# Two tiles of a layer's gathers replaced by products of adjacency blocks, in a graph network's second layer

## The reference

```python
deg = segment_sum(ones, dst)                 # with a loop at each node
dinv = rsqrt(deg);  norm_edge = dinv[src] * dinv[dst]
for W, b in ((W1, b1), (W2, b2), (W3, b3)):
    msg = (h @ W)[src] * norm_edge[:, None]
    h = relu(segment_sum(msg, dst) + b)
out = layernorm(x + h)
```

## Time and profile before

| | |
|---|---|
| median of three runs | 2339.77 us (2338.68 to 2342.82) |
| the profiled execution | 2341.41 us |
| its span, from its first to its last instruction | 2339.7 us, mean granted TensorE clock 0.972 |
| TensorE busy in matmuls, over the span | 2150.6 us, 92% |
| GpSimd busy, over the span | 1696.3 us, 73% |
| ScalarE, VectorE busy | 740.3 us (32%), 867.4 us (37%) |
| moved in all | 551.88 MB, 236 GB/s |

### The profile page before, as it was taken

How to read it: one execution, slowest core, us unless ns; L and a number is a source line. 1 busy time by engine, 2 the same in 40 slices (tenths; PEclk the granted TensorE clock), 3 DMA queues, 4 the chain that set the end, 5 groups by cost and what they waited for, 6 DMA issues and landing times.

```text
span 2339.7 us, 33336 instructions
## 1 busy us (share of the span) xinstructions
PE 2150.6 (92%) x10765; PEld 1430.9 (61%) x10765; DVE 867.4 (37%) x1213; ACT 740.3 (32%) x1578; POOL 1696.3 (73%) x1768
## 2 busy tenths in 40 slices
PE   5777999999999998899998999999899899999998
PEld 4755677777777774444444444444444368888886
DVE  8888322222222212233333333333332234444443
ACT  7611222323332312232322323322231134444443
POOL 4177777777777776777777777777777777777774
PEclk9788999999999999999999999999999999999999
DMA  7445767667766676888887888888888788888995
GB/s 229 142 122 183 235 201 210 207 210 211 209 206 208 209 210 194 246 259 264 258 261 250 258 264 257 262 245 255 260 257 278 230 259 264 266 265 295 313 317 163
DMA packets 238443, 551.88 MB, mean 236 GB/s; under 512 B 39676, under 2 KB 110451, under 8 KB 238307
## 3 DMA queue, kind: packets, MB, share of 16 engines
q0 software_dynamic: 124608, 395.36, 56.0%
q1 hardware_dynamic: 91011, 121.92, 15.2%
q10 hardware_dynamic: 22688, 32.75, 4.3%
HBM read 463.88 MB, written 86.00 MB: 235 GB/s over the span
## 4 chain that ended last, share of the span: by engine, by line
PE 58%; POOL 16%; issue 13%; DMA 7%; DVE 5%; POOLq 1%; ACTq 0%; DVEq 0%; ACT 0%; SPq 0%
POOL rows L778 15%; PE ps_acc L1756 8%; PE ps_o L1812 7%; PE ps_T L1851 7%; PE ps_h L1851 7%; PE ps_acc L1752 6%; PE ps_d L1862 6%; PE ps_d L1756 6%; DMA rows<-table,idx 5%; PE ps_h L1801 3%; DVE big L941 1%; PE ps_acc L1745 1%; PE ps_acc L1748 1%; PE ps_d L1748 1%; PE ps_d L1745 1%
## 5 line engine op out<-in xcount | busy, mean ns | idle before, releaser
L778 POOL DMA_INDIRECT rows<-table,idx x1018 | 985.3, 968 | 328.9 <-issue 292.0
L1756 PE MATMUL ps_acc<-rows,sel 128*128 128x512 f32 (+2 forms) x1122 | 496.3, 570 | 81.8 <-DMA rows<-table,idx 60.8
L778 POOL DMA_INDIRECT rows<-table_parts,idx x483 | 457.0, 946 | 147.2 <-issue 136.8
L998 DVE SCALAR_TENSOR_TENSOR sel<-ps_e,firsts,dstT 128x1152 f32<-128x1152 f32 (+1 forms) x174 | 246.1, 1414 | 614.5 <-PE ps_acc L1756 213.9
L1756 PE MATMUL ps_d<-rows,sel 128*128 128x512 f32 (+1 forms) x850 | 411.0, 607 | 34.9 <-DMA rows<-table,idx 34.8
L1756 PEld LDWEIGHTS ps_acc<-rows,sel 128*128 128x128 f32 x1122 | 206.6, 202 | 233.4 <-issue 143.7
L778 POOL DMA_INDIRECT rows_r<-table_pairs,idx x231 | 220.0, 952 | 72.1 <-issue 65.3
L1812 PE MATMUL ps_o<-low,hT 128*128 128x512 f32 (+1 forms) x784 | 270.5, 488 | 0.5 <-ACT hT L1432 0.5
L1752 PE MATMUL ps_acc<-rows,sel 128*128 128x256 bf16 (+1 forms) x1533 | 242.8, 274 | 16.9 <-DVE acc L1088 8.3
L1756 PEld LDWEIGHTS ps_d<-rows,sel 128*128 128x128 f32 x850 | 147.5, 191 | 171.2 <-issue 116.0
L1525 ACT ACTIVATE rows_r<-low 128x1280 fp32r<-128x1280 uint8 (+3 forms) x140 | 175.3, 1252 | 187.2 <-PE ps_T L1851 77.2
(11 more groups left out here) (211 smaller groups left out, 2122.8 us busy)
## 6 DMA issues: line engine op xcount, KB each, us to landing
rows<-table,idx POOLq DMA_INDIRECT x1018, 4.0
low<-built ACTq DMA_DIRECT2D x40, 320.0 KB, 4.9
table<-made SPq DMA_DIRECT2D x49, 256.0 KB, 3.1
acc<-table SPq DMA_DIRECT2D x49, 256.0 KB
table_pairs<-made_r SPq DMA_DIRECT2D x49, 256.0 KB
built<-big SPq DMA_DIRECT2D x30, 384.0 KB, 3.7
low<-built_bytes ACTq DMA_DIRECT2D x72, 160.0 KB, 4.0
built_bytes<-big SPq DMA_DIRECT2D x54, 192.0 KB, 4.9
```

The lines of the kernel that those rows point to most:

```text
L778: pool.indirect_dma_start(out=to, out_offset=None, in_=its[0:nodes, :], in_offset=bass.IndirectOffsetOnAxis(ap=idx[:, of, k:k + 1], axis=0 ...
L998: v.scalar_tensor_tensor(to[:, k:k + FRONT, :], numbers.unsqueeze(1).broadcast_to([P, FRONT, P]), firsts[:, bass.ds(t, 1)], dstT[:, bass.d ...
L1756: return mm(to[:, 0:w], sel[:, k, :], rows_of[phase][:, k, 0:w] if first is None else first, start=start, stop=stop)
```

## The change

Tiles 44 and 45 of layer 2 are no longer gathered. Their sums are made in windows 1 to 43, in 49 steps (h = 0 to 48). A step multiplies two 128x128 blocks of counts (one of each tile) with tile h of the layer's table (128x512, fp32) and adds into two PSUM banks, `ps_h` and `ps_o`. A window has one step, at slots 11 and 12 of its order; the six windows without a build have a second one, at 14 and 15. The table's tile is loaded from HBM by SP a window ahead, into two buffers. The counts are loaded in strips of six blocks for each tile, also two buffers, and widened from bf16 to fp32 by ScalarE, one activation of 128x256 a step, between the scaling of a sum and the copies of the build steps. Buffers lie in parts of the build buffers that layer 2, building bytes, leaves unused.

`ps_o` being taken, the products with W3 write into `ps_T`, the bank of the transposes. So it is the turn that now waits for the pair of the product before, and a product waits for all of `hT` at once. `make` and `make_pair` read `ps_T`.

The windows of layer 2 are 0 to 43 and three more, for tiles 46, 47 and 48. The one for tile 46 starts afresh. Turn and product of 44 and 45 are put into the windows of 46 and 47, beside those of the tile before. In layer 3 the two banks of the dense tiles are `ps_h` and `ps_o`, where they were `ps_T` and `ps_h`.

```diff
+AT_2 = (11, 14)
+TWO_PLACES = (3, 7, 7)
+DENSE_2 = (44, 45)
+STRIP = 6
+    GATHER_2 = T - len(DENSE_2)
+    WINDOWS = [0, GATHER_1, GATHER_1 + GATHER_2]
-        ps_dense = [ps_T[:, :], ps_h[:, :]]
+        ps_dense = [ps_h[:, :], ps_o[:, :]]
...
+        TWICE = [ROUND * i + o + 1 for i in range(ROUNDS) for o in range(ROUND) if half_in(o) is None]
+        STEPS_2, at_step = [[]], 0
+        for i in range(1, DENSE_2[0]):
+            STEPS_2.append(list(range(at_step, at_step + (2 if i in TWICE else 1))))
+            at_step += len(STEPS_2[i])
...  SP
+                    def strip(q):
+                        if q > 1:
+                            sp.wait_ge(widened_2, STRIP * (q - 1))
+                        lo_h, hi_h = q * STRIP, min((q + 1) * STRIP, T)
+                        for d, t in enumerate(DENSE_2):
+                            sp.dma_start(strips[:, q % 2, d, 0:(hi_h - lo_h) * P],
+                                         built[(t - GATHER) * P:(t - GATHER + 1) * P, lo_h * P:hi_h * P]).then_inc(strips_in[q % 2], 16)
+                    def loads_2(i):
+                        for h in STEPS_2[i]:
+                            if h > 1:
+                                sp.wait_ge(dense_2_step, h - 1)
+                            sp.dma_start(rows_2[:, h % 2, :], table[1][h * P:(h + 1) * P, :]).then_inc(rows_2_in[h % 2], 16)
+                            if h % STRIP == 0 and 0 < h and h + STRIP < T:
+                                strip(h // STRIP + 1)
...
                                 own_rows(t)
+                                loads_2(t + 1)
                                 stores(i, o, first)
                                 store(t - 1, nth(1, t - 1))
...
+                        strip(0)
+                        strip(1)
+                        loads_2(1)
                         round_of(0, True)
...  VectorE
-                v.scalar_tensor_tensor(made_r[:, C:2 * C], ps_o[:, 0:C], dinv[:, t:t + 1], made_r[:, 0:C].bitcast(F32),
+                v.scalar_tensor_tensor(made_r[:, C:2 * C], ps_T[:, 0:C], dinv[:, t:t + 1], made_r[:, 0:C].bitcast(F32),
...
+                last_pairs = [(DENSE_2[0] - 3,), (DENSE_2[0] - 2, DENSE_2[0] - 1), DENSE_2, (DENSE_2[1] + 1,)]
...
+                            v_.wait_ge(dense_2_step, T)
...  ScalarE
+            def scale_dense_2(d):
+                s = nth(1, DENSE_2[d])
+                act.wait_ge(dense_2_step, T)
+                act.wait_ge(turned, s)
+                act.sem_inc(act_step, 1)
+                nc.scalar.activation(aggT[:, 0:HID], ps_dense[d], ACT.Copy, scale=dinv[:, DENSE_2[d]:DENSE_2[d] + 1]).then_inc(agg_ready, 1)
+            def widen_2(h):
+                act.wait_ge(strips_in[h // STRIP % 2], 32 * (h // STRIP // 2 + 1))
+                if h > 1:
+                    act.wait_ge(dense_2_step, h - 1)
+                act.sem_inc(act_step, 1)
+                at = h % STRIP * P
+                nc.scalar.activation(counts_2[:, h % 2, :, :], strips[:, h // STRIP % 2, :, at:at + P], ACT.Copy).then_inc(widened_2, 1)
...
+            def tile(phase, t, n, s, per, built_half=None, between=None):
+                scale(phase, t, n, s, per)
+                if phase == 1 and per == 1:
+                    for h in STEPS_2[t + 1] if t + 1 < len(STEPS_2) else []:
+                        widen_2(h)
+                behind_scale(phase, t, s, per, built_half, between)
...  TensorE
-            def turn(phase, s, of=agg, at=0):
+            def turn(phase, s, of=agg, at=0, pairs=0):
                 pe.wait_ge(agg_ready, s + 1)
+                if pairs > 0:
+                    pe.wait_ge(pair_made, pairs)
...
-            def product(phase, s, pairs=0):
+            def product(phase, s, to=ps_o):
...
-                if pairs > 0:
-                    pe.wait_ge(pair_made, pairs)
+                if to is ps_T:
+                    pe.wait_ge(hT_ready, KH * s + KH)
...
+                def dense_2(h, d):
+                    if d == 0:
+                        pe.wait_ge(rows_2_in[h % 2], 16 * (h // 2 + 1))
+                        pe.wait_ge(widened_2, h + 1)
+                    ins = mm(ps_dense[d], counts_2[:, h % 2, d, :], rows_2[:, h % 2, :], start=h == 0, stop=h == T - 1)
+                    if d == 1:
+                        ins.then_inc(dense_2_step, 1)
+                def flow_beside(t):
+                    def beside(k):
+                        at = ORDER.index(k)
+                        if at == 10:
+                            turn(1, nth(1, t), aggT if t in DENSE_2 else agg, pairs=t)
+                        if at == 14:
+                            product(1, nth(1, t), ps_T)
+                    return beside
...
+                i = DENSE_2[0]
+                steady(1, i, TWO_PLACES, flow_beside(i), s=nth(1, i - 1), ps=ps_sums[(WINDOWS[1] + i) % 2], afresh=5, tile=tile_in(i))
+                i += 1
+                steady(1, i, TWO_PLACES, flow_beside(i + 1), s=nth(1, i), ps=ps_sums[(WINDOWS[1] + i) % 2], tile=tile_in(i), of=aggT)
+                i += 1
+                steady(1, i, LAST_PLACES[1], s=nth(1, T - 2), ps=ps_sums[(WINDOWS[1] + i) % 2], tile=tile_in(i))
```

More of the change, by code:

```diff
@@ L449, in gnn_program @@
         dense_taken = sem("dense_taken")
+        rows_2_in = [sem(f"rows_2_in{b}") for b in range(2)]
+        strips_in = [sem(f"strips_in{b}") for b in range(2)]
+        widened_2 = sem("widened_2")
+        dense_2_step = sem("dense_2_step")
         res_d_in = sem("res_d_in")
@@ L508, in in_bytes, with tile_in @@
             return not DENSE - DENSE_1 - 1 <= j < DENSE - 1
+        def tile_in(i):
+            return i if i < DENSE_2[0] else i + len(DENSE_2)
+        TWICE = [ROUND * i + o + 1 for i in range(ROUNDS) for o in range(ROUND) if half_in(o) is None]
[3 more added lines that the diff above has]
+            at_step += len(STEPS_2[i])
+        assert at_step == T and DENSE_2[0] == ROUND * ROUNDS + 2 and GATHER_2 == DENSE_2[0] + 3
+        assert all(not in_bytes(t - GATHER) for t in DENSE_2)
         def nth_window(phase, t, per, w):
@@ L692, in phases @@
                             round_of(i)
[L693 to L701, removed]
+                        last_flows = [(DENSE_2[0] - 2,), (DENSE_2[0] - 1, DENSE_2[0]), (DENSE_2[1], DENSE_2[1] + 1), (T - 2,)]
+                        for o, flows in enumerate(last_flows):
+                            i = ROUND * ROUNDS + o + 1
+                            own_rows(tile_in(i), nth_of_windows(1, i), late=i < GATHER_2 - 1)
+                            if o < 2:
+                                stores(ROUNDS, o)
+                            for t in flows:
+                                store(t, nth(1, t))
                         store(T - 1, nth(1, T - 1))
@@ L858, in one_window @@
                     else:
-                        with pool.Fori(0, (GATHER_1, T, GATHER)[phase] // 2) as i:
+                        with pool.Fori(0, (GATHER_1, DENSE_2[0] - 1, GATHER)[phase] // 2) as i:
                             two(i)
+                        if phase == 1:
+                            for i in range(DENSE_2[0] - 1, GATHER_2):
+                                t = tile_in(i)
+                                need = pool.value_load(need_i[0:1, t:t + 1], min_val=0, max_val=99)
+                                window(1, nth_of_windows(1, i), nth_of_windows(1, i) % 2, need, afresh=i == DENSE_2[0])
             def sweeps():
@@ L1178, in one_window, with steady @@
             def one_window():
[L1179 removed]
+                def steady(phase, t, odd, hots=None, whole=None, units=None, last=False, in_parts=False, tile=None, next_tile=None, dense=None, pairs=()):
                     n = nth_of_windows(phase, t)
@@ L1199, in steady @@
                     prepare(n, t, base, 1, sel_parts if in_parts else sel_r if phase == 2 else sel)
-                    if phase == 1 and t > 1:
-                        make_pair(t - 2)
+                    for made_tile in pairs:
+                        make_pair(made_tile)
                 def to_next(phase):
@@ L1446, in make @@
                 act.wait_ge(o_done, s + 1)
+                of = ps_T if phase == 1 and per == 1 else ps_o
                 if phase == 1 and per == 1:
@@ L1614, in first_pieces @@
                         widen(0, x)
-                for t in range(ROUND * ROUNDS, T):
-                    tile(1, t, nth_of_windows(1, t), nth(1, t), 1, between=first_pieces if t == T - 1 else None)
+                for t in range(ROUND * ROUNDS, DENSE_2[0] - 1):
+                    tile(1, t, nth_of_windows(1, t), nth(1, t), 1)
+                t = DENSE_2[0] - 1
+                scale(1, t, nth_of_windows(1, t), nth(1, t), 1)
+                behind_scale(1, t, nth(1, t), 1)
+                scale_dense_2(0)
+                behind_scale(1, DENSE_2[0], nth(1, DENSE_2[0]), 1)
+                scale_dense_2(1)
+                behind_scale(1, DENSE_2[1], nth(1, DENSE_2[1]), 1)
```

(2 more changed lines are left out.)

77 lines of the change are left out of this document (48 added, 29 removed).

## The result

The changed kernel takes 2303.88 us in the median of four runs (2302.12 to 2304.87); the kernel before took 2341.3 us in four runs beside it. The ratio is 0.9836, with a 95% interval from 0.9824 to 0.9848: 37.4 us or 1.6% faster, where 2306 us was forecast. The profiled execution spans 2301.9 us at a mean granted clock of 0.981.

What follows compares the result with a forecast made beforehand. GpSimd's gathers were taken to bound layer 2, TensorE close behind: 2341.4 us, less 38 for gathers removed, plus 4 for the longer stretch, less 1.6 from profiled execution to median, gave 2306 us, range 2300 to 2327.

Steps and rivals of the forecast that it cites:

- GpSimd bounds layer 2, and the gain is its gathers: Layer 2: GpSimd issues gathers without pause, one every 1.260 us; 31 fewer save 36.5 to 39.1 us, 38 taken.
- 91 us free on TensorE, not 62: Windows 1 to 43: TensorE's counted work is 777 of 868 us, leaving 91 free; its busy row shows only 62.
- the window without waits: Layer 2, 1004.04 to 1022.38 us before the change: TensorE waited for nothing, 18.34 us product to product, used for pricing.
- Dense steps, 84.4 us, hidden: Windows 1 to 43: 98 added matmuls at 0.861 us cost TensorE 84.4 us, covered by its 91 free.
- Widening, 7 us of TensorE: ScalarE, before the build copies: 49 activations of 0.5 us delay TensorE by 4 to 14 us, 7 taken.
- Shared bank, nothing: Layer 2's turn, waiting for the pair of the previous product: about 3.4 us in hand with builds, so no cost.
- Loads hidden: SP's queue in layer 2: 16.1 MB of added block and strip loads make no store later.
- the transfers' rival: Layer 2: SP's loads delay gathers if engines sustain under 265 GB/s; 62 us more at 258, 2364 us; chance 0.11.
- Start, 2 us of TensorE, nothing for GpSimd: Window 0: 1.05 MB of loads leaving at once delay TensorE 0 to 4 us, 2 taken, GpSimd not at all.
- The end, hidden: Windows of 46 and 47: turn and product of tiles 44 and 45 are hidden by GpSimd; uncovered, 4.2 us.
- The sum, 872 for the stretch: Windows 1 to 43: TensorE 870 us, GpSimd 868, so about 872 where 868 stood, +4 (bounds 0 and +16).
- nothing lost: Whole kernel, rival: TensorE keeps within GpSimd's pace, the lag absorbed; 2301 us (2298 to 2302), chance 0.10.

Runs made afterwards that it cites:

- relieving TensorE of 81 us: Changed kernel without the matmuls of 47 of the 49 dense steps, their loads and widening kept: 2303.07 us, 0.9847 of the kernel before.
- relieving GpSimd of 58: Changed kernel without the gather of slot 14 in 46 windows of layer 2, stale rows multiplied instead: 2292.55 us, 0.9799 of the kernel before.
- the loaded kernel: Changed kernel with the product of tile 44 made twice in each dense step, 42.2 us more TensorE work: 2336.8 us, 0.9991 of the kernel before.
- the changed kernel's repeat: The changed kernel run again without any edit, as base for the other runs: 2302.28 us, 0.9836 of the kernel before.
- the doubled loads: Changed kernel with 45 of the 49 table blocks loaded a second time into an unused buffer, 11.8 MB more: 2307.73 us, 0.9861 of the kernel before.
- the kernel with early strips: Changed kernel with the first two count strips of both tiles loaded at layer 1's end instead of during window 0: 2305.26 us, 0.9847 of the kernel before.

## Why the prediction was right, step by step

- **GpSimd bounds layer 2, and the gain is its gathers.** Right. From the first gather of layer 2 to the first of layer 3, GpSimd took 996.05 us for 787 gathers before and 959.08 us for 756 after: 31 fewer, 37.0 us less, between the two ways of 36.5 and 39.1; 38 was taken. Relieving TensorE of 81 us changed nothing, and relieving GpSimd of 58 gave 10 us of time, and no more because TensorE stood there.
- **91 us free on TensorE, not 62.** Right, and the step on which the sign hung. The relieved GpSimd let TensorE's work be seen: 860.4 us, against 861.4 from the window without waits. By the busy row 22 us would have been lost; none were. The Trainium skill (Perfetto Trace Analysis, Identifying the Most-Contended Engine) points to the weight loads instead. The trace agrees that there was room: they were busy 392.25 us before and 428.27 after. Their share alone doesn't say how much, since TensorE is nearly full after with 49%. Set against the window without waits, in which they were busy 9.30 of 18.34 us, the 392.25 us stand for 774 us of work, near the 777 counted.
- **Dense steps, 84.4 us, hidden.** Right: 0.86 us each, 7 us left over by the prediction; by the runs 868.06 - 860.36 = 7.7, and the loaded kernel absorbed 8.
- **Widening, 7 us of TensorE.** Mis-sized: it costs TensorE nothing that can be measured. The activation does come between scaling and first copy, 0.41 us each, and the weight load of the third build step does wait longer (0.50 us in window 5). But the matmul behind it isn't later: from one build step to the next there are 1007.86 - 1006.81 = 1.05 us, with 1.06 before. The kernel in which TensorE alone sets the pace has the widening too, and its windows are no longer for it (20.06 us). The prediction had put only 0.1 us in hand there; there was more.
- **Shared bank, nothing.** Right. Alone it cost no time, and where TensorE set the pace the turn wasn't seen to wait for the pair.
- **Loads hidden; the transfers' rival.** Right: 275 GB/s in the stretch, past the 265 from which that rival was to fall, and 289 when forced. The waits for gathered rows fell, as quoted above. The Trainium skill (DMA: Bandwidth & Descriptors, Queues, rings and completion order) states that the DMA engines take turns between queues; no run here shows a price of that. The landing of a gather, 5.0 us in the median before, is 3.9 us in the changed kernel's repeat and 5.0 us with the doubled loads, so it doesn't follow the transfers. The profile knows the landing of few gathers only (43 of 689 before, 87 in each of the other two; a single one in the profile after).
- **Start, 2 us of TensorE, nothing for GpSimd.** Window 0 is 2.9 us longer in the profile after, and 4.9 in that of its repeat (36.20). None of it is on the path. In that repeat GpSimd is never idle for more than 0.4 us between two gathers, from the first of layer 2 to the first of layer 3, and they take 960.35 us, 959.08 in the profile after, and 958.43 in the kernel with early strips, whose window 0 was the longest of the three. Why TensorE's first sum comes later isn't settled, since the run made for it missed.
- **The end, hidden.** Right in that nothing was lost. The three windows are 2.2 us shorter, which no step had: two gathers fewer were left for them, as told with the table, 2.5 us of GpSimd's work. That is the lag given back, and no gain of its own.
- **The sum, 872 for the stretch.** Mis-sized, following from the widening and the start: +0.06 us where +4 stood. Without these two terms the sum is 2302, the edge to "nothing lost", and the measured 2303.9 lies between the two. That it lies so near to 2306 is in part luck: the gathers gave 37.0 us where 38 was taken, and the stretch lost nothing where 4 was taken. GpSimd's "first real waits" didn't come either, for the same reason.

What stays open is why TensorE's sum of window 0 comes 2 to 6 us later in the changed kernel and its variants, which costs no time, and the small excess of the doubled loads.

## What to carry to other kernels

Count what an engine has left from a stretch in which it waits for nothing, product to product, and not from its busy row, which counts tails and low clock as work; here 91 against 62 us decided the sign. Work moved from the pacing engine to one with room is free until both are level, and not further: here 42 us more on TensorE cost 34.5, and 58 us less on GpSimd gave 10. To see how far one stands from that point, relieve each engine alone and then both; only the last gives the gain.

## What had not been expected

The 1.260 us of a gather is an average of two things. Gathers in clear stretches start every 1.25 us; the rest is four gathers beside VectorE's `take_apart`. The two of window 17 after, with VectorE's copy and subtraction (start, length, operation, wait before):

```profile
1246.83 2.34 POOL L828 DMA_INDIRECT rows<-table,idx  x1 [0.30 <-PE ps_acc L1846]
1247.31 1.75 DVE L1198 CAST pairs_r<-big 128x3072 fp32r<-128x3072 f32 x1
1249.10 3.36 DVE L1200 TENSOR_TENSOR pairs_r<-big,pairs_r 128x3072 fp32r<-128x3072 f32 x1
1249.48 3.79 POOL L828 DMA_INDIRECT rows<-table,idx  x1 [0.30 <-issue]
```

The first gather ends 0.11 us after the end of the copy (1249.17 to 1249.06), the second 0.81 us after the subtraction (1253.27 to 1252.46), instead of after 0.95 us. With window 31 (1.92 and 3.79 us) that is 2.34 + 3.79 + 1.92 + 3.79 - 4 x 0.95 = 8.0 us, and 688 x 1.25 + 8.0 = 868.0 is the stretch. So it was before, with shorter ones: 2.09 and 3.10 us at both places, 6.6 us more than 689 x 1.25 = 861.25, against the stretch of 868.00. There the gather beside the copy ends 0.81 us behind it too (1245.48 + 2.09 = 1247.57 to 1244.87 + 1.89 = 1246.76). It started after the copy, where the one of 2.34 us had started before: in these cases a gather that starts second ends 0.8 us behind VectorE, nearly its whole 0.95 us. With the copy on ScalarE the gathers beside it are short, and one long one is left in each window, ending 0.82 us after the subtraction:

```profile
1251.09 2.78 ACT L1693 ACTIVATE pairs_r<-big 128x3072 fp32r<-128x3072 f32 x1
...
1252.29 0.94 POOL L828 DMA_INDIRECT rows<-table,idx  x1 [0.30 <-issue]
...
1253.97 3.36 DVE L1201 TENSOR_TENSOR pairs_r<-big,pairs_r 128x3072 fp32r<-128x3072 f32 x1 [7.32 <-ACT pairs_r L1693]
1254.79 3.36 POOL L828 DMA_INDIRECT rows<-table,idx  x1 [0.30 <-issue]
```

The Trainium skill (SBUF — State Buffer, SBUF: two separate sides) states that VectorE and GpSimd share a pair of ports, that certain operations of VectorE, a copy of fp32 among them, hold it for the whole instruction, and that a DMA issued from GpSimd can't write its descriptors meanwhile. For the copy both traces agree: the gather ends behind VectorE's instruction, and a copy on ScalarE doesn't hold the gather. For the subtraction it is only seen that the gather beside it is long and ends 0.8 us behind it; no run moved it.

GpSimd alone pays these 8 us, and they are most of what puts the stretch above TensorE's work: 688 x 1.25 = 860.0 us of clear gathers stand against 860.4 us of TensorE's work. Window by window, the changed kernel is longer than the one with fewer gathers by 1.89 and 1.04 us in windows 17 and 18, by 1.93 and 1.27 in 31 and 32, and by 1.35 in 43; the other 38 together make 0.2. What could return as time is bounded by the 7.7 us that TensorE has left.
